# Two products of the identity with the constants ahead of each transposed norm

## What is computed

```
for layer in (0, 1):
    x = x + gate * (attention(norm(x) @ Wqkv) @ Wo)         # self attention
    x = x + attention(norm(x) @ Wq, context @ Wkv) @ Wo     # cross attention
    x = x + gate * (gelu(norm(x) @ W1) @ W2)                # MLP, 128 -> 512 -> 128
```

## Time and profile before

| | |
|---|---|
| time, median of 3 runs | 483.98 us (481.41 to 486.79) |
| the profiled execution | 484.73 us |
| its span, first to last instruction | 482.9 us |
| mean granted TensorE clock | 0.897 |
| busy: PE, DVE, ACT, POOL | 391.4, 330.1, 267.9, 159.0 us |

### The profile page before, as it was taken

How to read it: one execution, slowest core, us unless ns; L and a number is a source line. 1 busy time by engine, 2 the same in 40 slices (tenths; PEclk the granted TensorE clock), 3 DMA queues, 4 the chain that set the end, 5 groups by cost and what they waited for, 6 DMA issues and landing times.

```text
span 482.9 us, 9958 instructions
## 1 busy us (share of the span) xinstructions
PE 391.4 (81%) x3744; PEld 240.0 (50%) x3744; DVE 330.1 (68%) x841; ACT 267.9 (55%) x503; POOL 159.0 (33%) x138
## 2 busy tenths in 40 slices
PE   1555889888889797797987887989889898979686
PEld 1422455556555544434534534556565554737464
DVE  2656768999999837728648736799999884721331
ACT  1112457667676664565475554576576665666552
POOL 4764263455283401701601601335154161020130
PEclk9965599999999997978899958799999897979989
DMA  8860837558584516124225213346657551420001
GB/s 251 288 196 0 237 87 213 162 177 231 142 213 141 131 69 126 48 90 106 71 92 101 76 71 90 84 150 167 155 156 191 150 141 69 114 42 23 3 1 44
DMA packets 31271, 59.20 MB, mean 123 GB/s; under 512 B 3455, under 2 KB 7807, under 8 KB 30975
## 3 DMA queue, kind: packets, MB, share of 16 engines
q1 hardware_dynamic: 30935, 58.35, 43.9%
q10 hardware_dynamic: 288, 0.21, 0.2%
HBM read 31.81 MB, written 26.74 MB: 121 GB/s over the span
## 4 chain that ended last, share of the span: by engine, by line
PE 47%; DVE 21%; ACT 11%; POOL 9%; issue 5%; DMA 4%; SPq 2%; ACTq 0%; DVEq 0%; POOLq 0%
DVE maxima L683 8%; PE ps_misc L992 8%; PE ps_ao L966 8%; PE ps_misc L911 7%; POOL Kd L763 6%; PE ps_sc L949 6%; DVE xn L588 5%; PE ps_misc L1012 5%; ACT PT L843 5%; PE ps_misc L873 4%; ACT xnT L829 4%; PE ps_misc L998 3%; PE ps_misc L929 2%; POOL rstd L747 2%; DVE stats L578 2%
## 5 line engine op out<-in xcount | busy, mean ns | idle before, releaser
L843 ACT ACTIVATE PT<-ps_sc 128x512 f32<-128x512 f32 (+1 forms) x256 | 138.9, 596 | 79.8 <-PE ps_sc L949 79.0
L683 DVE TENSOR_REDUCE maxima<-ps_misc 128x4 f32<-128x512 f32 (+1 forms) x256 | 154.1, 666 | 29.4 <-PE ps_misc L929 29.1
L763 POOL TENSOR_SCALAR Kd<-Kh,head_rows 128x512 fp32r<-128x512 f32 (+1 forms) x64 | 98.6, 1556 | 114.2 <-ACT Kh L803 87.4
L949 PE MATMUL ps_sc<-Qd,Ks 57*128 57x256 f32 (+1 forms) x512 | 65.7, 335 | 18.6 <-ACT PT L843 15.6
L966 PE MATMUL ps_ao<-PT,V 120*18 120x128 f32 (+1 forms) x2048 | 71.6, 279 | 2.8 <-ACT PT L843 2.7
L744 POOL TENSOR_SCALAR vareps<-mv 128x4 f32<-128x4 f32 (+1 forms) x28 | 6.8, 242 | 188.5 <-DVE mv L581 188.0
L949 PEld LDWEIGHTS ps_sc<-Qd,Ks 57*128 57x128 f32 (+1 forms) x512 | 38.6, 187 | 55.7 <-ACT PT L843 28.4
L966 PEld LDWEIGHTS ps_ao<-PT,V 120*18 120x18 f32 (+1 forms) x2048 | 50.7, 99 | 20.9 <-issue 9.6
L829 ACT ACTIVATE xnT<-ps_misc,vec 128x128 f32<-128x128 f32 x80 | 30.1, 458 | 45.5 <-PE ps_misc L873 33.7
L911 PE MATMUL ps_misc<-xnT,W 128*128 128x512 f32 x72 | 47.5, 784 | 5.1 <-ACT xnT L829 5.1
L929 PE MATMUL ps_misc<-Kd,Qh 32*128 32x512 f32 (+1 forms) x256 | 45.3, 535 | 7.6 <-POOL Kd L763 6.5
(11 more groups left out here) (75 smaller groups left out, 455.2 us busy)
## 6 DMA issues: line engine op xcount, KB each, us to landing
Qd<-q_mem SPq DMA_DIRECT2D x64, 192.0 KB
k_mem<-Kh SPq DMA_DIRECT2D x16, 512.0 KB, 3.2
q_mem<-Qh SPq DMA_DIRECT2D x16, 512.0 KB, 3.4
Ks<-k_mem SPq DMA_DIRECT2D x32, 192.0 KB
Ks<-k_mem SPq DMA_DIRECT2D x32, 180.0 KB
k_mem<-Kl SPq DMA_DIRECT2D x16, 256.0 KB, 3.6
q_mem<-Ql SPq DMA_DIRECT2D x16, 256.0 KB, 2.9
W<-weights SPq DMA_DIRECT2D x1, 1792.0 KB, 18.9
```

The costliest lines, as they stand in the source:

```text
L683: dve.tensor_reduce(maxima[:, HG * n:HG * n + HG, st.b], bank(st.use + n)[:, 0:HG * ns].rearrange("p (h k) -> p h k", h=HG), AX_X, ALU.max ...
L763: pool.tensor_scalar(Kd[:, st.f % 2, c, 0:n], f32(Kh[:, st.f % 2, 0:n]), head_rows[:, c:c + 1], None, ALU.mult).then_inc(S["kd_ready"], 1)
L843: act.activation(PT[0:ns, st.k % PSLOTS, g, :, :, :].rearrange("p i e t -> p (i e t)"), ps_sc[0:ns, g, :], ACT.Exp, scale=SCALE).then_inc( ...
L949: ins = pe.matmul(ps_sc[0:ns, side, i * E * P:(i + 1) * E * P], Ks[rows, st.f % 2, n, st.b * ns:(st.b + 1) * ns], Qd[rows, st.f % 2, n, :, ...
```

## The change

Each `xT` step gets two products after its `fill` and ahead of its wait for `xn_ready`. Each product takes the identity as stationary and all 384 columns of `cst` as moving operand, and writes the first 384 columns of the bank that the four transposes then overwrite. Nothing reads what the products write. No semaphore is added, and no other step changes its place.

```
+WARM = 2
...
+                def warm(use):
+
+                    for _ in range(WARM):
+                        pe.matmul(bank(use)[:, 0:NCONST], ident, cst[:, :], start=True, stop=True)
...
                     if st.kind == "xT":
                         fill(st.use)
+                        warm(st.use)
                         pe.wait_ge(S["xn_ready"], CB * (st.k + 1))
                         turn(xn, st.use)
```

## The result

The changed kernel takes 481.86 us in the median of 20 runs (475.6 to 486.9), the kernel before 484.75 us in 20 runs beside it (481.1 to 488.2). The ratio is 0.9887, 95% interval 0.9854 to 0.9919, so it is faster by about 1%. The ratio takes only the runs within 1.5% of each kernel's fastest, 11 of the 20 of the changed kernel and all 20 of the one before; over all runs the medians give 0.994 and the means 0.993 (0.990 to 0.996). The forecast was 486 us, a hair slower.

A forecast was written before the change was run, and what follows sets the result against it. In the dense middle the bound was PE's order with ACT and DVE beside it; slow half-clock products also lay on the chain. 484.7 + 15.9 cost - 14.7 gain = 485.9, forecast 486 us, range 476 to 495.

The forecast's parts named there:

- The price of a pair: Two 384-column products on PE at an xT step: 1.3 us at full clock, 2.6 at half clock.
- The cost: What pairs stick out behind PE's waits, summed over all steps: 15.9 us, bounds 5.6 and 18.
- The gain: Chain time saved where the pairs hold the clock up: 14.7 us of 23.4 for ten falls, bounds 0 and 23.4.
- 185.3, 226.2, 263.8: Half-clock stretches starting at these us, whose wait the pair fills whole: taken as gone, 5.9 us together.
- 205.8, 400.3: Half-clock stretches behind steps 10 and 20, priced 3.05 and 2.6 us; wait filled in part, two thirds saved.
- 297.9: Half-clock stretch from 297.9 us, begun ahead of or beside a step; priced 2.8 us, half saved.
- 383.3: Half-clock stretch from 383.3 us, begun ahead of or beside a step; priced 1.5 us, half saved.
- 458.4: Half-clock stretch from 458.4 us, priced 1.1 us on the chain; claimed to stay, nothing saved.
- All falls go: Rival, chance 0.2: any work in the gap may be enough, all 23.4 us saved; 477.2 us.
- The clock doesn't answer: Rival, chance 0.2, with falls only moving: 5.9 us or less saved, 494.7 us; nothing saved, 500.6.
- The dense units absorb: Rival, chance 0.1: DVE bounds the dense units, so 10.3 of 15.9 us cost nothing; 475.6 us.
- The falls cost more than the chain shows: Rival, chance 0.12: every PE product in a fall may be waited for, 30 us to win, 19 won; 481.7 us.

The follow-up runs named there:

- dense pairs only: Pair of products only at the thirteen other steps (1 to 8, 16 to 19, 22), none at the eleven long waits; 496.71 us, ratio 1.0267 to the kernel before.

## Why the prediction was wrong, point by point

The time lies inside my range of 476 to 495, but I had forecast a kernel slightly slower than before, and it is faster. The step that failed is the gain, the share of the falls that go.

**What bounds the kernel** was read rightly: the waits of the earlier trace rows and the slow pieces of the earlier trace rows were where the gain lay, and the long first stretch stayed.

**The price of a pair** was right: 1.29 us at step 8 on the chain against 1.3 forecast, and 2.6 of delay at step 2, at half clock, against 2.6.

**The cost** was right within 1 to 2 us: 15.9 us forecast, the rest column has 15 to 16, the trace some 17. Steps 1 and 2 took 1.7 and 2.6, as forecast; steps 3 to 8 took 6.6 where 7.3 was forecast. For steps 16 to 19, where the bank's wait ends last, I had 3.0. After has 3.4, but a gain at step 16 is in it; with dense pairs only they took 4.4 (1.4, 0.8, 1.3 and 0.9, where I had 0.7, 1.25, 0.75 and 0.35). Step 22 was the one mis-sized: its pair stood on the chain with 2.28 us, at half clock, and I had 0.9. That DVE might absorb the pairs fell: the dense units took 20.3 us between steps 5 and 6 of after where it was 19.0.

**The gain is the term that was mis-sized**: 14.7 us forecast, about 19 measured (18.9 by the table; in the traces 17 of cost and 1.9 us less time). Its price was right (23.4 us for 65 us at half clock is 0.36 us each; the runs give 0.35). The share of the falls that go was too small. The prediction had the mean clock at 0.94, and it was 0.954: 0.014 x 332 = 4.6 us, more than the whole 2.9 that the change gained. Step by step, with what I gave each fall and what the traces have from that step to the next:

| fall | forecast | measured |
|---|---|---|
| 185.3, 226.2, 263.8 | 2.3, 1.9, 1.7 | 2.3, 2.3, 1.7 |
| 205.8, 400.3 | 2.0, 1.7 | 1.4, 1.0 |
| 277.4 | 0.9 | 2.0 |
| 297.9 | 1.4 | 1.0 |
| 383.3 | 0.8 | 3.0 |
| 427.6 | 1.9 | 3.0 |
| 458.4 | 0 | 1.4 |

(297.9 is taken against the kernel with dense pairs only; to 427.6 the 2.28 us of step 22's pair are added.) So the falls that I counted as gone were sized nearly right. Of the three behind half-filled waits two were sized too high and one too low. Most of what was missing lies in the falls that I had kept for the greater part. The one at 383.3 gave twice its whole price of 1.5, and why is open. The one at 458.4 only moved: it came at 454.4, onto step 22's pair, so that its 1.4 us stand in the cost. I had set the shares by how much of the wait the pair fills. The trace shows that a fall can also get shorter: behind steps 10, 14 and 20 it is still there but lasts 3.4 us instead of 6.8 to 10.2, and the MLP's four products take 5.3 instead of 6.3 to 6.7. My own sign, L992 at 3.7 us in at least two of MLPs 1, 4 and 5, failed by this: only MLP 5 had it. I gave step 14 a quarter of its 3.5 us, and its piece alone won 1.5. The fall at 297.9, 10.2 us long, went, and only one of 3.4 us came at 317.9. A second piece, under 1 us, wasn't foreseen at all: the transposes start 0.09 us sooner when their wait is parted from the bank's.

**The rivals.** "All falls go" had named 477: the fastest runs are there (475.6), the median is not. "The clock doesn't answer" and "the falls only move" fell by the kernel with pairs in the waits only. "The dense units absorb" fell by its counterpart. "The falls cost more than the chain shows" had named 481.7, and 481.86 was measured; that is luck. Its price is 0.46 us for each us at half clock (30 for 65), so the 51 us less would be 24, and with 17 of cost the time 478. The penalty rule of the Trainium skill ("TensorE: Matmul & The Clock Gate", Terms), half of the throttled time, doesn't agree with the runs here: they give 0.35 us for each us. That not all that PE does at half clock is waited for would explain it: at 185.3 PE was busy for 6.39 us and the chain had 2.3 to win. By its 0.5 the 51 us less at half clock in the profile would be 26 us, by 0.35 they are 18. Here it was the smaller number that fitted.

**The sum** is a small difference of two large terms. With both near 15 us, a tenth of one is half of what was to be forecast; the sign hung on the share of falls, for which the trace of before had no row.

## What to carry to other kernels

Where TensorE's granted clock dips behind short waits, products into a bank that will be overwritten can hold it up if they lie inside the wait (0.945 here, where it was 0.897). Look for each place which wait ends last, for a product that is queued behind the late one, or in a unit without a wait, is paid in full. Put them at the places with a wait and not at the others: here that made 1% into 4%. Price a fall by its length and not as there or gone. Where two large terms nearly cancel, forecast the two of them and call the sign open.

## What the runs showed of the hardware that was not expected

Work on 32 rows and 32 columns kept PE as busy as the full products (1.47 and 1.46 us a pair) but the mean clock was 0.914, with the full ones 0.945, with none 0.897.

A PE instruction that waited for the bank and then for `xn` started 146 ns behind the end of `xn` (twelve starts in the kernel before); with only the wait for `xn` on it, it started 55 ns behind (eleven starts with the 16 columns ahead). Two waits alone don't make it: where the first of the two ended last, as at one of steps 16 to 19 before, it was 56 ns.

A product of 16 columns between two waits made the kernel 0.7% faster; behind both it made it 0.8% slower. Of the 8.4 us between the two, each against its own runs of the kernel before, some 4 go with the clock (0.904 and 0.891) and about 1 is the sooner start; the rest, and why the clock differs, is open.
